# Masked attention loop entered after 14 row maxima instead of 18, with half of the query spreads moved into its steps

## The chip, the cores and the metric

The kernel runs on one core of a Trainium2 chip. The metric is the device time of one execution in microseconds (us), as the median of several runs. The engines named are PE (TensorE), DVE (VectorE), ACT (ScalarE), POOL (GpSimd) and SP (SyncE, which here only issues DMAs).

## The reference, cut to what matters

The program is a two-layer decoder on x of shape (2, 256, 128) with a context of shape (2, 512, 128). Layer 0 is a state-space mixer, a cross attention and a mixture of experts; layer 1 a latent self attention (called "a" in the kernel), a masked cross attention ("x") and a mixture of experts. Each block adds its result to x and normalizes. The change touches the seam of the two attentions of layer 1:

```python
x = layernorm(x + L1_attn(x))                      # "a": 16 heads of 8, 256 keys
# "x": 16 heads of 8, 512 keys, two batch entries
q = einsum('bse,ehd->bhsd', x, Wq) + bq
k = einsum('bse,ehd->bhsd', ctx, Wk) + bk
logits = where(mask, -1e8, einsum('bhsd,bhtd->bhst', q, k))
attn = einsum('bhst,bhtd->bhsd', softmax(logits), v) / sqrt(8)
x = layernorm(x + einsum('bhsd,hdo->bso', attn, Wo) + bo)
```

## The kernel before

Everything is written out by hand: each engine has its own program, and semaphores (`S[...]`) tie them together. An engine waits in the order of its own program, so a wait holds back all that stands behind it. PSUM has 8 banks of 128 x 512 floats.

**The two attention loops.** A loop (`attend_a`, `attend_x` in each engine's program) goes over steps n, a step being 4 heads and 128 keys. In step n PE makes the logits of step n + 1 (keys on partitions, into banks 0 to 3), ACT takes their exponentials (`exp_late`), and PE multiplies the exponentials of step n with the values (`values`, bank 4 or 5). "a" has 16 steps, "x" 32. After the last key tile of a group of 4 heads DVE copies the sum out (`kept`). For "x" PE also adds the mask by two bf16 products with `neg_i` in each half of the logits.

**The maxima.** So that exponentials stay in range, the greatest logit of every query row must be known before the loop reaches its head. PE therefore makes the logits a second time with the queries on partitions (`rows`, one 128x512 matmul for "x"), DVE reduces each to a maximum (`row_max`, for "x" a custom instruction at L1411 that adds the mask and takes the maximum, and a short read of the accumulator). When 8 of these "row" slots of "x" (4 heads of one entry) are done, a "max" slot follows: PE turns the maxima (`max_cols`), ACT copies them negated (`minus_max`), POOL splits them into three bf16 parts (`minus_parts`, 4 instructions), and SP sends each part by DMA into the stacked queries `qs` (`spread_max`). `logits` of the first step of that group waits for the three DMAs. "x" has 64 row slots r0 to r63 and 8 max slots m0 to m7; m0 is for steps 0 to 3, m1 for steps 4 to 7, and so on.

**Where the slots stand.** `first_slots` are those ahead of the loop, 18 rows for "x" (`AHEAD`), in the banks 6, 7, 2, 3 in turn, the last two in 6 and 7; `later_slots` stand in the steps, three to a step until they are used up, in banks 6 and 7 in turn. In a step of "x" PE's order is: slot, half of the logits, slot, other half, slot, values. A slot waits until the one before it in its bank has been read (`fill_slot` and `used`): for a row, until DVE has its maximum. Ahead of the loop each row slot has one identity matmul ahead of it, work without use that keeps PE busy (`idle_work`).

**The spreads.** The queries of "x" are stored as three bf16 parts side by side. `query_parts` (DVE) splits the product of `queries` (PE), 12 small copies per entry (`gather_four`, three by DVE, nine by POOL) bring 4 heads each to the same partitions, and 8 "spreads" per entry (`spread_x`: two 96-row matmuls on PE, one 128x512 copy on ACT) lay two heads each out in `qs`. Entry 0 is batch 0. Before the change all 16 spreads stand ahead of the loop, between its first rows (`spreads_x`), and the loop waits for all.

**The seam.** At the end of loop "a", entry 0 has been attended and normalized (`a_summed(0)`, `a_scaled(0)`, POOL's `root`); entry 1's last heads are copied out, turned (`out_rows`), divided (`normed_rows`), turned again (`attended_cols`), multiplied with Wo (`attended_rows`), summed with the residual (`a_summed(1)`), normalized (`a_scaled(1)`) and turned for the query product (`half_cols("a", 1)`, `queries(1)`). `SECOND` names the row slots of "x" beside which the later pieces of entry 1 stand, `BESIDE` the steps of a loop beside which the pieces of entry 0 stand, `TURNED` the step at which entry 0's attended heads are turned and divided. After the loop of "x" comes the expert layer.

The line of the matmuls is L1666 for all (the helper `mm`).

## Time and profile before

| | us |
|---|---|
| runs (3) | 461.35, 462.95, 464.19 |
| median | 462.95 |
| the profiled execution | 461.53 |
| its span, first to last instruction | 459.7 |

1.83 us of the profiled execution lie outside its span. In a timeline row the columns are: start, length, engine, line, operation, result <- operands, (partitions*columns of the weights) elements and type, how many instructions are merged; in brackets how long the engine stood idle before and what released it. The length of a matmul includes its way through the array, so the starts of neighbouring rows give PE's pace. "PEld" is the load of weights, which overlaps the matmuls.

### The profile page before, as it was taken

The page shows a single profiled execution, that of the slowest core. Times are in us where ns is not written, and L with a number is a line of the kernel's source. Part 1 is how long each engine was busy: PE and PEld are TensorE (multiplying, and loading weights), DVE is VectorE, ACT ScalarE, POOL GpSimd, SP SyncE. Part 2 cuts the span into 40 slices and gives each one's busy share as a digit, 9 for nine tenths or more (in the row PEclk, how much of TensorE's full clock was granted, in tenths as well). Part 3 has the DMA queues.
Part 4 walks back from the last instruction along what each step waited for, and adds up shares of the span by engine and source line. Part 5 has one row for each costly group of instructions (what it writes and reads, how often), then busy time and mean ns, then how long its engine had stood idle before and what let it go on. Part 6 is the DMA issues. An engine that isn't in the chain of part 4 may idle for free.

```text
span 459.7 us, 7702 instructions
## 1 busy us (share of the span) xinstructions
PE 414.8 (90%) x2878; PEld 273.4 (59%) x2886; DVE 294.2 (64%) x688; ACT 206.1 (45%) x290; POOL 185.9 (40%) x237
## 2 busy tenths in 40 slices
PE   4898999999999999798999986789869999999985
PEld 4676645444554447475799864544546555658975
DVE  4779976777666675431622788464688886246644
ACT  1676623233333333115423376457346554566550
POOL 3316647787676766310050465421263332200000
PEclk9989999999999999989999999799999999999998
DMA  8712000000004111160054004300000000000000
GB/s 314 287 37 79 1 0 2 1 1 0 1 1 182 47 46 47 54 223 7 1 133 62 2 0 66 45 3 3 0 1 3 2 2 3 2 13 25 0 1 23
DMA packets 8080, 19.78 MB, mean 43 GB/s; under 512 B 1958, under 2 KB 3974, under 8 KB 7526
## 3 DMA queue, kind: packets, MB, share of 16 engines
q1 hardware_dynamic: 8044, 19.30, 14.3%
q8 instruction: 23, 0.38, 0.3%
q14 instruction: 13, 0.11, 0.1%
HBM read 17.26 MB, written 1.15 MB: 40 GB/s over the span
## 4 chain that ended last, share of the span: by engine, by line
PE 65%; DVE 15%; issue 5%; POOL 5%; DMA 5%; ACT 3%; another core or an unknown queue 0%; SPq 0%; POOLq 0%; DVEq 0%; ACTq 0%
PE ps L1666 63%; DMA late<-mid 4%; DVE ps L1411 3%; DVE big L1215 2%; POOL big L695 2%; DVE ps L1210 2%; DVE mx_a L1415 1%; DMA ident<-in_ident 1%; DVE big L1287 1%; POOL big L702 1%; DVE big L1278 1%; PE ps L1678 1%; POOL big L651 1%; PE ps L2115 1%; ACT late L1061 0%
## 5 line engine op out<-in xcount | busy, mean ns | idle before, releaser
L1666 PE MATMUL ps<-big,late 128*32 128x256 f32 (+3 forms) x760 | 96.7, 383 | 3.0 <-DVE mx_a L1415 1.5
L1666 PE MATMUL ps<-late,big 128*128 128x128 f32 (+1 forms) x448 | 65.6, 277 | 2.6 <-DMA late<-mid 1.9
L955 ACT ACTIVATE big<-ps 128x1024 f32<-128x1024 f32 x48 | 49.1, 1024 | 39.8 <-PE ps L1666 39.6
L894 ACT ACTIVATE big<-ps 128x1024 f32<-128x1024 f32 x32 | 32.8, 1025 | 65.2 <-PE ps L1666 56.8
L1666 PEld LDWEIGHTS ps<-big,late 128*32 128x32 f32 (+2 forms) x768 | 35.0, 116 | 41.4 <-issue 18.4
L1666 PEld LDWEIGHTS ps<-late,big 128*128 128x128 f32 (+1 forms) x448 | 47.2, 152 | 20.1 <-issue 13.3
L695 POOL TENSOR_TENSOR big<-big 128x512 f32<-128x512 f32 x32 | 41.1, 1285 | 28.1 <-DVE big L1287 28.1
L1287 DVE TENSOR_SCALAR big<-big 128x1024 f32<-128x1024 f32 x32 | 27.7, 866 | 33.2 <-ACT big L894 33.2
L1411 DVE CUSTOM_DVE_ANT_0 ps<-ps,big 128x512 f32<-128x512 f32 x64 | 42.7, 708 | 6.9 <-remote 3.2
L630 POOL TENSOR_SCALAR vareps<-meanvar 128x2 f32<-128x2 f32 (+2 forms) x13 | 3.0, 228 | 104.5 <-DVE meanvar L1109 100.7
L1666 PE MATMUL ps<-ident 128*128 128x128 f32 x194 | 28.3, 290 | 7.1 <-DMA ident<-in_ident 6.5
L917 ACT ACTIVATE big<-ps 128x512 f32<-128x512 f32 x32 | 18.9, 597 | 34.0 <-PE ps L1666 34.0
L1666 PE MATMUL ps<-ctx_r,attn_w 128*128 128x512 f32 x64 | 32.6, 618 | 0.7 <-ACT late L861 0.7
L1666 PEld LDWEIGHTS ps<-ident 128*128 128x128 f32 x194 | 26.3, 206 | 8.1 <-DMA ident<-in_ident 6.5
L1666 PE MATMUL ps<-xT,late 128*128 128x256 f32 (+1 forms) x96 | 29.9, 452 | 1.3 <-ACT big L917 1.3
L1666 PE MATMUL ps<-attn_w,ctx_r 128*128 128x128 f32 (+1 forms) x192 | 29.7, 289 | 0.4 <-ACT late L968 0.3
L1666 PE MATMUL ps<-attn_w,big 128*128 128x128 f32 x192 | 26.5, 285 | 2.9 <-DVE big L1279 2.3
L1278 DVE RECIPROCAL big<-ps 128x256 f32<-128x256 f32 x16 | 28.0, 1748 | 1.3 <-PE ps L1666 1.3
L1666 PEld LDWEIGHTS ps<-attn_w,ctx_r 128*128 128x128 f32 (+1 forms) x192 | 23.9, 171 | 7.6 <-issue 2.9
L651 POOL TENSOR_TENSOR big<-big,mid 128x512 f32<-128x512 f32 x16 | 20.4, 1274 | 19.7 <-DVE big L1215 19.7
L1666 PEld LDWEIGHTS ps<-attn_w,big 128*128 128x128 f32 x192 | 24.3, 197 | 5.9 <-DVE big L1279 2.8
L1666 PE MATMUL ps<-big,mid 64*128 64x256 f32 x192 | 27.2, 402 | 0.0
(261 smaller groups left out, 721.2 us busy)
## 6 DMA issues: line engine op xcount, KB each, us to landing
attn_w<-in_w_x SPq DMA_DIRECT2D x1, 2560.0 KB, 12.4
big<-parts_kx SPq DMA_DIRECT2D x18, 128.0 KB
late<-in_w_up SPq DMA_DIRECT2D x1, 2048.0 KB, 7.5
late<-in_w_dn SPq DMA_DIRECT2D x4, 512.0 KB, 4.0
attn_w<-in_w_up SPq DMA_DIRECT2D x1, 1024.0 KB, 7.7
attn_w<-in_w_dn SPq DMA_DIRECT2D x1, 1024.0 KB, 10.1
big<-mid SPq DMA_DIRECT2D x24, 32.0 KB, 1.8
parts_kx<-ctx_r SPq DMA_DIRECT2D x1, 768.0 KB, 3.2
```

The lines of the kernel that those rows point to most:

```text
L651: nc.gpsimd.tensor_tensor(hC[:, s % 8, :], hs[:, s % 4, :], Cn[:], ALU.mult).then_inc(S["hC_done"], 1)
L695: nc.gpsimd.tensor_tensor(esum[:, s, :].rearrange("p (r t) -> p r t", r=2), e[:, :, 0, :], e[:, :, 1, :], ALU.add).then_inc(S["e0_sum"], 1)
L702: nc.gpsimd.tensor_tensor(etot[:, b, :], esum[:, 0, :], esum[:, 1, :], ALU.add).then_inc(S["e0_tot"], 1)
L894: nc.scalar.activation(ex[:, n % 3, :].rearrange("p (r n) -> p r n", r=2), ps[:, 2 * (n % 2):2 * (n % 2) + 2, :], ACT.Exp).then_inc(S["e0_ ...
L917: nc.scalar.activation(dst, ps[:, up_bank0(k, c), :], ACT.Gelu).then_inc(S["up0_act"], 1)
L955: nc.scalar.activation(ex1[:, n % 3, :].rearrange("p (r n) -> p r n", r=2), ps[:, 2 * (n % 2):2 * (n % 2) + 2, :], ACT.Exp, scale=scale).t ...
L1210: nc.vector.tensor_tensor(dBx, dBx, Bn[:], ALU.mult).then_inc(S["dBx_done"], 1)
L1215: nc.vector.tensor_tensor_scan(hs[:, s % 4, :], dA[:, s % 2, :], dBx, 0.0, ALU.mult, ALU.add).then_inc(S["scan_done"], 1)
L1278: link(nc.vector.reciprocal(dst, ps[:, 4 + b, T:2 * T]))
L1287: nc.vector.tensor_scalar(ex[:, n % 3, :], ex[:, n % 3, :], float(np.exp(CLIP)), float(np.exp(-CLIP)), ALU.min, ALU.max).then_inc(S["e0_cl ...
L1411: nc.vector.tensor_tensor_reduce(ps[:, bank, :], ps[:, bank, :], mq[:, 2 * b + q, :], 1.0, -FAR, ALU.add, ALU.max, dst).then_inc(S[f"{L}_r ...
L1666: return nc.tensor.matmul(o, lhsT, rhs, start=start, stop=stop, skip_group_check=shared)
```

## The change

It does these things:

- 14 rows of "x" stand ahead of the loop in place of 18, and m0 with them; m1 moves into step 1. The others go into the steps at the same rate as before.
- Entry 1's 8 spreads stand in the loop, one as the first slot of each of the steps 0 to 7, in bank 6 or 7; the first 8 stay ahead of it. Steps 0 to 7 so have 4 slots. The slots' banks still go 6, 7, 6, 7.
- At the end of loop "a", entry 0's chain to its query (`half_cols("a", 0)`, `queries(0)`, `query_parts(0)`) goes ahead of entry 1's last heads. Entry 1's pieces go beside the first rows of "x": `attended_cols` at row 1, `attended_rows` and `a_summed` at row 3, `half_cols` and `a_scaled` at row 5, `queries` at row 7, `query_parts` at row 8. The 8 identity matmuls ahead of the first spread are gone.
- POOL splits m0 ahead of the nine gathers of entry 1 and not behind them, and it adds the residual's bias behind these.
- Later in loop "x" entry 0's pieces move: turned at step 21 (19), `aT` 22 (20), `y` 23 (21), `xT` 25 (24), router 26 (25).

```diff
-        AHEAD = {"a": 16, "x": 18}
+        AHEAD = {"a": 16, "x": 14}
...
-                if L == "x" and m % row_steps(L) == 1 and m > 1:
+                if L == "x" and m % row_steps(L) == 0 and m:
                     slots.append(("max", m // row_steps(L) - 1))
...
+                if L == "x" and n < H // 2:
+                    slots.append((n, ("spread", H // 2 + n)))
...
-        TURNED = {"a": 9, "x": 19}
-        BESIDE = {"a": {"aT": 11, "y": 12}, "x": {"aT": 20, "y": 21, "xT": 24, "router": 25}}
+        TURNED = {"a": 9, "x": 21}
+        BESIDE = {"a": {"aT": 11, "y": 12, "xT": 15}, "x": {"aT": 22, "y": 23, "xT": 25, "router": 26}}
...
-            return [m - 2] if 8 <= m < AHEAD["x"] else [2 + m // 2] if m % 2 else []
+            return [2 + m // 2] if m % 2 and m < H - 4 else []
...
-        SECOND = {"xT": 1, "q": 3, "parts": 5}
+        SECOND = {"aT": 1, "y": 3, "xT": 5, "q": 7, "parts": 8}
...
             root("post3_0")
             gather_four("qx", 0, 1)
+            gather_four("qx", 0, 2)
             root("post3_1")
-            gather_four("qx", 0, 2)
             gather_four("qx", 0, 3)
+            minus_parts("x", 0)
             pool.wait_ge(norm_out, normed_tiles("post3_1"))
-            nc.gpsimd.tensor_tensor(resid[:], x[:], rv4("bo1"), ALU.add).then_inc(S["res_ready"], 1)
-            pool.wait_ge(S["res_ready"], 5)
             for f in (1, 2, 3):
                 gather_four("qx", 1, f)
-            for k in range(groups("x")):
+            nc.gpsimd.tensor_tensor(resid[:], x[:], rv4("bo1"), ALU.add).then_inc(S["res_ready"], 1)
+            for k in range(1, groups("x")):
                 minus_parts("x", k)
...
@ attend_x, PE
-                half_cols("a", 0)
-                out_rows("a", 1, (H // 4 - 1,))
                 queries(0)
-                attended_cols("a", 1)
-                attended_rows("a", 1)
-                idle_work(2, 8)
                 pe.wait_ge(S["a_o_sb"], 2 * (H // 4))
                 for n in spreads_x(-1):
                     spread_x(n, 4 + n % 2)
+                out_rows("a", 1, (H // 4 - 1,))
...
-                pe.wait_ge(S["x_spread"], H)
+                pe.wait_ge(S["x_spread"], H // 2)
...
@ DVE
                     if n == B * (H // 4) * KEYS["a"] // P - 1:
                         a_scaled(0)
+                        query_parts(0)
                     kept("a", n)
...
             attend_a()
-            query_parts(0)
-            a_summed(1)
             attend_x(1.0 / float(np.sqrt(np.float32(DH))))
```

PE at the end of loop "a", step 15, before. `ident,mid` are `out_rows`, `big2,late` the values, `ident,x` is `half_cols`, `xT,w_x1` `queries`, `ident,x2` `attended_cols`, `w_a1,w_mix` `attended_rows`, `attn_w,ctx_r` a spread, `big1,late` a row.

```order
L2115 MATMUL ps<-ident,mid 128x128 x6
L1666 MATMUL ps<-big2,late 32x256 x4
L2143 MATMUL ps<-ident,x 128x128 x2
L2115 MATMUL ps<-ident,mid 128x128 x2
L1666 MATMUL ps<-xT,w_x1 128x256
L2124 MATMUL ps<-ident,x2 128x128 x2
L1666 MATMUL ps<-w_a1,w_mix 128x128 x2
L1666 MATMUL ps<-ident 128x128 x8
L1666 MATMUL ps<-attn_w,ctx_r 128x256 x4
```

The same place after the change.

```order
L2154 MATMUL ps<-ident,x 128x128 x2
L2126 MATMUL ps<-ident,mid 128x128 x6
L1673 MATMUL ps<-big2,late 32x256 x4
L1673 MATMUL ps<-xT,w_x1 128x256
L1673 MATMUL ps<-attn_w,ctx_r 128x256 x4
L2126 MATMUL ps<-ident,mid 128x128 x2
L1673 MATMUL ps<-ident 128x128
L1673 MATMUL ps<-big1,late 128x512
```

`half_cols` has moved ahead of the first six turns and the values; the first spreads are ahead of entry 1's last two turns.

PE in step 0 of loop "x" before: three rows, and `late,big1` with `sel,neg_i` are a half of the logits.

```order
L1666 MATMUL ps<-big1,late 128x512
L1666 MATMUL ps<-late,big1 128x256 x2
L1666 MATMUL ps<-sel,neg_i 128x256 x2
L1666 MATMUL ps<-big1,late 128x512
L1666 MATMUL ps<-late,big1 128x256 x2
L1666 MATMUL ps<-sel,neg_i 128x256 x2
L1666 MATMUL ps<-big1,late 128x512
L1666 MATMUL ps<-big2,late 32x256 x4
```

Step 0 after the change.

```order
L1673 MATMUL ps<-attn_w,ctx_r 128x256 x2
L1673 MATMUL ps<-late,big1 128x256 x2
L1673 MATMUL ps<-sel,neg_i 128x256 x2
L1673 MATMUL ps<-big1,late 128x512
L1673 MATMUL ps<-late,big1 128x256 x2
L1673 MATMUL ps<-sel,neg_i 128x256 x2
L1673 MATMUL ps<-big1,late 128x512 x2
L1673 MATMUL ps<-big2,late 32x256 x4
```

The spread has the place of the first row, and the last two slots stand side by side.

POOL around the splits, before: `attn_w<-ctx_r` are gathers (three to a call), `resid` the residual's bias, then the split of m0 and of m1.

```order
L630 TENSOR_SCALAR vareps<-meanvar 128x2
L632 TENSOR_TENSOR rstd<-vareps,neghalf 128x2
L730 COPY attn_w<-ctx_r 32x256 x6
L781 TENSOR_TENSOR resid<-x,rowv 128x512
L730 COPY attn_w<-ctx_r 32x256 x9
L742 CAST mid<-mid 4x256
L744 TENSOR_TENSOR mid<-mid 4x256
L745 CAST mid<-mid 4x256
L747 TENSOR_TENSOR mid<-mid 4x256
```

After.

```order
L632 TENSOR_SCALAR vareps<-meanvar 128x2
L634 TENSOR_TENSOR rstd<-vareps,neghalf 128x2
L732 COPY attn_w<-ctx_r 32x256 x3
L744 CAST mid<-mid 4x256
L746 TENSOR_TENSOR mid<-mid 4x256
L747 CAST mid<-mid 4x256
L749 TENSOR_TENSOR mid<-mid 4x256
L732 COPY attn_w<-ctx_r 32x256 x9
L786 TENSOR_TENSOR resid<-x,rowv 128x512
```

The split of m0 is ahead of nine gathers.

## Rows read from the trace of the kernel before

**Rows 1.** The page, part 4: the chain that ended last.

```profile
PE 65%; DVE 15%; issue 5%; POOL 5%; DMA 5%; ACT 3%; another core or an unknown queue 0%; SPq 0%; POOLq 0%; DVEq 0%; ACTq 0%
```

**Rows 2.** Windows: stretch and length, busy of PE, PEld, DVE, ACT, POOL, clock, DMA.

```profile
326.50:332.50 6.00, 4.52 (x32) 3.66 (x34) 4.78 (x17) 1.46 (x4) 1.40 (x4) 1.00 0.00 0
...
341.00:345.00 4.00, 1.74 (x14) 1.50 (x16) 3.96 (x13) 1.28 (x4) 3.44 (x10) 1.00 0.00 0
...
350.16:367.72 17.56, 17.20 (x153) 9.21 (x153) 15.08 (x44) 9.38 (x11) 6.29 (x12) 1.00 0.01 3
```

**Rows 3.** Timeline of PE, end of loop "a" to the first spread.

```profile
324.66 0.88 PE L2115 MATMUL ps<-ident,mid 128*128 128x128 f32 x6
...
327.00 0.65 PE L1666 MATMUL ps<-xT,w_x 128*128 128x256 f32 x2
...
331.39 0.60 PE L1666 MATMUL ps<-attn_w,ctx_r 96*128 96x256 bf16 x4
```

**Rows 4.** Timeline of DVE, the seam up to the first row maximum.

```profile
324.95 0.60 DVE L1119 TENSOR_SCALAR x<-summed,meanvar,rstd 128x128 f32<-128x128 f32 x2 [0.69 <-POOL rstd L632]
326.24 0.42 DVE L1441 COPY mid<-ps 128x256 f32<-128x256 f32 x1 [0.69 <-PE ps L1666]
...
328.01 0.47 DVE L1132 TENSOR_SCALAR ctx_r<-ps,vec 128x256 bf16<-128x256 f32 x1
...
330.88 0.43 DVE L1448 TENSOR_TENSOR summed<-ps,resid 128x256 f32<-128x256 f32 x1
...
333.01 0.70 DVE L1411 CUSTOM_DVE_ANT_0 ps<-ps,big 128x512 f32<-128x512 f32 x1 [0.91 <-remote]
```

**Rows 5.** Timeline of DVE, then PE: r15 and r17 share bank 6.

```profile
347.46 0.73 DVE L1411 CUSTOM_DVE_ANT_0 ps<-ps,big 128x512 f32<-128x512 f32 x1
...
349.05 0.70 DVE L1411 CUSTOM_DVE_ANT_0 ps<-ps,big 128x512 f32<-128x512 f32 x1
```

**Rows 6.** Timeline of PE: r17 with its identity, first logits, values of two later steps.

```profile
348.31 0.49 PE L1666 MATMUL ps<-ident 128*128 128x128 f32 x2
348.63 0.38 PE L1666 MATMUL ps<-big,late 128*128 128x512 bf16 x1
...
349.29 0.38 PE L1666 MATMUL ps<-late,big 128*128 128x256 bf16 x2
...
389.16 0.64 PE L1666 MATMUL ps<-big,late 128*32 128x256 f32 x8
...
390.71 0.64 PE L1666 MATMUL ps<-big,late 128*32 128x256 f32 x8
```

**Rows 7.** Chain of waits, from a negated maximum to the logits that need it.

```profile
314.73 0.37 ACT mid L1011
...
317.50 1.76 DMA late<-mid
...
319.40 0.60 PE ps L1666 x4
```

**Rows 8.** Timeline of ACT, then POOL: two spreads copied, exponentials of step 0; nine gathers, then the split.

```profile
331.81 1.08 ACT L1002 ACTIVATE late<-ps 128x512 bf16<-128x512 f32 x2 [2.81 <-PE ps L1666]
...
350.36 1.02 ACT L955 ACTIVATE big<-ps 128x1024 f32<-128x1024 f32 x1 [0.24 <-PE ps L1666]
...
340.77 4.03 POOL L730 COPY attn_w<-ctx_r 32x256 bf16<-32x256 bf16 x9 [3.39 <-DVE ctx_r L1137]
```

**Rows 9.** Timeline of PE, then DVE: m7, entry 0's pieces in loop "x".

```profile
387.98 0.38 PE L2038 MATMUL ps<-ident,mx_x 128*4 128x128 f32 x2 [0.42 <-DVE mx_x L1411]
...
395.12 0.44 PE L2124 MATMUL ps<-ident,x 128*128 128x128 f32 x2 [0.36 <-DVE x L1428]
...
397.59 0.43 DVE L1529 TENSOR_TENSOR summed<-ps,resid 128x256 f32<-128x256 f32 x1 [2.53 <-PE ps L1666]
```

**Rows 10.** Windows, columns as in rows 2: two stretches at the start of loop "a".

```profile
296.00:298.00 2.00, 0.46 (x4) 0.30 (x4) 0.69 (x1) 0.30 (x2) 1.43 (x3) 0.73 0.00 0
298.00:300.00 2.00, 2.00 (x11) 1.34 (x9) 0.06 (x1) 1.34 (x2) 1.89 (x3) 0.50 0.02 4
```

More of the change, by code:

```diff
@@ L1023, in attend_x @@
                         spread_x(n, 4 + n % 2)
+                    if i == SECOND["aT"]:
+                        attended_cols("a", 1)
                     if i == SECOND["xT"]:
@@ L1030, in attend_x @@
                             minus_max("x", i, bank)
+                    for (kind, i), bank in slots_beside("x", n):
+                        if kind == "spread":
+                            spread_x(i, bank)
                     if n == BESIDE["x"]["aT"] + 1:
@@ L1499, in attend_x @@
                         row_max("x", i, bank)
+                        if i == SECOND["y"]:
+                            a_summed(1)
                         if i == SECOND["xT"]:
@@ L2015, in used @@
                     pe.wait_ge(S[f"{L}_redmax"], i + 1)
+                elif kind == "spread":
+                    pe.wait_ge(S["x_spread"], i + 1)
                 else:
@@ L2063, in fill_slot @@
                     rows(L, i, bank)
+                elif kind == "spread":
+                    spread_x(i, bank)
                 else:
@@ L2193, in attend_a @@
                         attended_cols("a", 0)
+                    if n == BESIDE["a"]["xT"]:
+                        half_cols("a", 0)
                     if n == total - 1:
@@ L2202, in attend_x @@
                 total = B * (H // 4) * KEYS["x"] // P
-                half_cols("a", 0)
-                out_rows("a", 1, (H // 4 - 1,))
                 queries(0)
-                attended_cols("a", 1)
-                attended_rows("a", 1)
-                idle_work(2, 8)
                 pe.wait_ge(S["a_o_sb"], 2 * (H // 4))
@@ L2220, in attend_x @@
                             spread_x(n, 4 + n % 2)
+                        if slot[1] == SECOND["aT"]:
+                            attended_cols("a", 1)
+                        if slot[1] == SECOND["y"]:
+                            attended_rows("a", 1)
                         if slot[1] == SECOND["xT"]:
```

## The prediction

> **What bounds the kernel now.** I read the page first: PE holds 65% of the chain that ended last [rows 1], so what counts is what PE has to wait for or to do more. Then the windows around the change. From 326.5 to 332.5 PE is busy 4.52 of 6.00 us, and 2 us of that are the 8 identity matmuls; from 341 to 345 it is busy 1.74 of 4.00 while DVE is busy 3.96 [rows 2]. So the stretch ahead of loop "x" goes at DVE's pace, a row maximum each 0.65 us. From 350.16 to 367.72 PE is busy 17.20 of 17.56 [rows 2]: these are steps 0 to 7 of loop "x", 17.56 / 8 = 2.195 us each, and there PE itself sets the pace. Steps with no slot are 390.71 - 389.16 = 1.55 us long [rows 6], so a slot costs PE (2.195 - 1.55) / 3 = 0.215 us. The change takes work and DVE time out of a stretch where PE waits and puts slots into one where PE is full. Last I read the timelines of PE and DVE at the seam and around r17, since they show the two turn-rounds used below.
>
> Two latencies. A row begun on PE at 348.63 is taken up by DVE at 349.05, 0.42 later [rows 5, 6]. The maximum of r15 began on DVE at 347.46; r17, in the same bank, was released by it, and its identity began on PE at 348.31, 0.85 later [rows 5, 6]. A bf16 row needs its weights loaded after the release, about 0.1 more (the identity and r17 lie 0.32 apart where their work is 0.22), so I take 0.93. From one row to the next in the same bank PE thus needs 0.42 + 0.93 = 1.35 us at least. Ordinary steps hardly feel this: slot 1 and slot 3 lie a row and two halves of logits apart, 2 x 0.215 + 2 x 0.435 = 1.30 (0.87 us is a step's logits, 350.16 - 349.29 from [rows 2, 6]).
>
> **Entry to loop "x".** Half_cols now stands where the six turns began, at 324.66 [rows 3]. It needs entry 0's rows, which DVE writes from 324.95 for 0.60 us [rows 4]; PE is through at about 325.85, then come the six turns (0.81) and the values (0.57), and the query product starts at about 327.2, against 327.00 [rows 3]. It takes 0.65, so DVE splits the query from 327.9, against 328.01 [rows 4]: the chain put first gains nearly nothing. Split and gather last until 330.88 in the row before, 2.87 us, now until 330.8; then the copy of entry 1's last heads, 0.42 [rows 4], and the first spreads start at 331.2, against 331.39 [rows 3]. They take 0.43, the last two turns 0.44. Before, the turns were issued by 327.00 and their division was over by 328.01, 1.0 us; so it is over at 333.1, and only then can DVE take r0. It took r0 at 333.01 [rows 4]. The eight identity matmuls (8 x 0.22) thus leave a wait, not time.
>
> From r0 on DVE has four row maxima less (-4 x 0.65 = -2.6) and the sum and statistics of entry 1 more (from 330.88 to 332.10, where the idle time ahead of r0 starts [rows 4]: +1.2). The stall behind the normalization of entry 1 stays. New: the last two slots are forced to banks 6 and 7, so r12 follows r11 in bank 6 with nothing between them. Before, r17 followed r15 with r16 between, and DVE took them up 1.59 apart [rows 5], which is 0.3 beyond two maxima; r12 comes 1.59 behind r11, 0.94 beyond one: +0.65. Sum -0.75, and with r0 0.1 later the last row is taken up near 348.4 instead of 349.05. But r17 was followed by a spread and m1 ahead of the first logits, and r13 is issued while DVE is still on r12. First logits at 349.29 before [rows 6], now about 347.7: **-1.6 us**. m0 does not hold them: it is made once r7 is reduced, near 341.4, its split no longer stands behind the 4.03 us of gathers [rows 8], and from the negated copy to the logits it is 319.40 - 314.73 = 4.67 us [rows 7], so they would be free at 346.5. Bounds of this term: 0 (if the 0.3 of the seam go wrong and DVE stalls twice more) and -3.0 (r0 a microsecond sooner, no wait at r12; then m0 is next).
>
> **In the steps.** (1) Eight spreads, four rows and m1 are 13 slots more: 13 x 0.215 = **+2.8**. PE is full there, nothing hides them.
>
> (2) In steps 0 to 7 slots 2 and 4 share a bank, and between their starts lie slot 2 itself, one half of the logits and slot 3: 0.215 + 0.435 + 0.215 = 0.87, against 1.35 needed. PE stands 0.48 before slot 4, in every one of these steps whatever it holds, since m1 and m3 wait for slot 2's maximum too. In step 0 the wait is another: ACT takes the exponentials of step 0 first, which begin 0.2 after the first slot (350.36 to 350.16) and last 1.02, and then copies the spread, 0.54 [rows 8]; slot 3 needs that copy, so it starts at about 1.85 in place of 1.30. That is 0.55, and 0.2 more at the start of step 1. Sum 7 x 0.48 + 0.75 = **+4.1**. Bounds: 0, since the same turn-round of 1.35 over 1.30 leaves no stall in [rows 2] (0.36 idle in 8 steps) and a 4-slot step is in no row; and 7 x 0.75 + 0.75 = 6.0, if DVE takes slot 2 half a maximum late each time. I stay by 0.48, since r17 shows it directly.
>
> (3) m1 moves from ahead of the loop to the last slot of step 1, and step 3 makes the first logits that need it. PE gets there 0.215 (m1) + 0.675 (values, 1.55 - 0.87) + 2.195 + 0.215 + 0.48 (step 2) + 0.215 (slot 1) = 4.0 us after it begins m1. The path needs 0.42 to ACT, some 0.1 behind an exponential, and the 4.67 of [rows 7]: 5.2. **+1.2**, all on PE, with DVE, ACT and the slots behind it queued. Bounds: 0 and 1.6. Later maxima have 2.75 steps or more.
>
> (4) At the end of the slots. m7 waited 0.42 for r63 [rows 9]; now it has a step to itself: **-0.4**. Entry 0's turned heads waited 0.36 [rows 9] because a copy of finished heads stands before the division in step 19; in step 21 there is none: **-0.35**. But `y` at step 23 puts such a copy ahead of the sum: the sum now waits for the values of step 23 (0.57) and the copy (0.42), 0.95 later than at 397.59 [rows 9], and half_cols has two steps instead of three. By the old offsets PE arrives 3.1 us after the sum may begin and its second tile was ready 3.05 after it; with the delay PE waits **+0.9**. Bounds -0.8 and +1.0 for all three. The router's chain ends a step later, ahead of matmuls that PE reaches 2 us after; 0.
>
> **Sum.** -1.6 + 2.8 + 4.1 + 1.2 - 0.4 - 0.35 + 0.9 = **+6.6 us**. The profiled execution took 461.53, 1.83 over its span: 468.1. It lies 1.4 below the median of the runs, 462.95; the mean of the four is 462.5, and on that the sum gives 469.1. I say **469.0**. Ends: -3.0 + 2.8 - 0.8 = -1.0 and 0 + 2.8 + 6.0 + 1.6 + 1.0 = +11.4.
>
> **The clock.** PE now idles from about 327.8 to 331.2, with no identity matmuls in between. Against a loss: from 341 to 345 it was busy 1.74 of 4.00 and the granted clock stayed at 1.00, 2.4 GHz [rows 2]. For it: with 0.46 us of work from 296 to 298 the clock fell, and from 298 to 300 it was 0.50, 1.2 GHz [rows 10]. So a fall is possible in the new gap. It would double spreads, turns, identity and r0 (0.43 + 0.44 + 0.44), about +1.3, the later rows being DVE's. The Trainium skill (TensorE: Matmul & The Clock Gate, "What's actually happening") says that the throttled state is the default and activity lifts it; by that rule this gap costs the 1.3, and the identity matmuls taken out had a use.
>
> **Rivals.** A, my sum: 469.0.
> B, the fourth slot is cheap: the wait of (2) does not show on PE, as the 1.35 over 1.30 does not now; only the slots, the m1 wait and the rest: -1.6 + 2.8 + 1.2 + 0.15 = +2.5, 465.0. For it: in the 8 steps PE idles only 0.36. Against: 0.48 is far more than 0.05.
> C, the clock falls in the seam: 469.0 + 1.3 = 470.3.
> D, not slower: the entry is what matters. If DVE meets no wait at r12 and takes r0 at 332, the loop is entered 3.0 earlier, at 346.3, and if slot 4 then also hides and neither m1's split nor half_cols is waited for: -3.0 + 2.8 - 0.75 = -0.95, 461.5 on the mean. It decides from an entry before 346.5 with steps 0 to 3 no longer than 2.45 us. For it: the 341 to 345 window, where PE idles 2.26. Against: it needs waits to vanish that [rows 5, 7] price.
>
> Chances: A 0.57, B 0.18, C 0.13, D 0.12. A range of 464.5 to 472.5 leaves out D's end and the high bound. About 1%, 4.6 us, is what a measurement here can tell from no change. A clears it but for its low tail (0.07), C clears it, B mostly not (0.03 of it does): slower 0.50 + 0.13 + 0.03 = 0.66; faster 0.03 from D's tail; the rest, 0.31, within.
>
> **What would show it.** In the trace after: first logits of "x" near 347.7; steps 1, 2, 4 to 7 about 2.89 us long with an idle PE of 0.4 to 0.5 before each fourth slot, released by DVE's maximum; a gap of about 1.2 in step 3 released by the DMA of m1; half_cols of entry 0 in step 25 waiting 0.9. I am wrong if PE stays busy over 95% in steps 0 to 7 (then B or D), if the first logits come before 346.5 (D), or if the granted clock is below 1 between 330 and 336 (C).

## The result and the profile after

| | before | after |
|---|---|---|
| median of the runs in one session | 463.57 us | 472.38 us |
| ratio | | 1.0212, interval 1.0135 to 1.0289 |
| the profiled execution / its span | 461.53 / 459.7 | 472.9 / 471.1 |

The change makes the kernel slower. The ratio is one of means (473.2 over 463.4 us): 2.1%, 9.8 us, or 8.6 without the run of 476.67; the medians lie 8.8 us apart. I had said slower, at 469.0, in a range that ended at 472.5. The median is at the very end of that range, and by the ratio the 462.95 from which I forecast becomes 472.8, beyond it. Executions far above the others of the same kernel (such as 1031.58 us in e11) are left out of all ratios here. The page of the profile of the kernel after, the clock by slices and the chain that ended last:

```profile
PEclk9999999999999999899999998799889999999999
...
PE 62%; DVE 13%; DMA 6%; POOL 6%; issue 5%; ACT 5%; SPq 1%; another core or an unknown queue 0%; DVEq 0%; POOLq 0%; ACTq 0%
```

The answer to [rows 1] is that PE holds less of the chain, 62% against 65%, and DVE too, 13% against 15%; ACT went from 3 to 5%, DMA and POOL from 5 to 6% each. I cut both executions at the same places (us from the start of the span), to see where the 11.4 us of the two spans lie:

| | before | after | difference |
|---|---|---|---|
| start of the span to the split of entry 0's query on DVE | 328.01 | 329.63 | +1.6 |
| from there to the first `neg_i` product of loop "x" | 21.49 | 23.50 | **+2.0** |
| from there to the first product with `w_sh`, behind the loop | 65.22 | 72.97 | **+7.75** |
| from there to the end | 45.0 | 45.0 | 0 |

The first difference is upstream of the change, and has two parts. The granted clock, which falls at the start of loop "a" in both kernels [rows 10], stayed at 0.50 longer: from 300 to 302 it was 0.50 after and 0.92 before, and by 307 the kernel after was 0.8 behind. Then a DMA landed later (2.74 us against the 1.76 of [rows 7]), which makes it 1.73. PE's timeline of the kernel after, the row that answers to the 319.40 of [rows 7]:

```profile
321.13 0.60 PE L1673 MATMUL ps<-late,big 128*128 128x256 bf16 x4 [1.30 <-DMA late<-mid]
```

It doesn't belong to the change: in a second execution of the same kernel (below, e10) the query split began at 328.17. From 1.73 at this row to 1.62 at the split the query chain, put first, gained 0.1, as forecast. The other two differences do. In these rows matmuls are L1673 (L1666 before), row maxima L1417 (L1411), turned maxima L2047 (L2038), `half_cols` L2154 (L2143).

**The entry.** The windows of the kernel after around the seam and around r12 (columns as in [rows 2]: busy time of each engine, granted clock, DMA):

```profile
330.00:332.00 2.00, 0.00 (x0) 0.00 (x0) 1.85 (x6) 0.00 (x0) 0.39 (x1) 1.00 0.00 0
332.00:334.00 2.00, 1.01 (x8) 0.97 (x8) 0.99 (x4) 0.58 (x2) 1.75 (x5) 0.91 0.00 0
334.00:336.00 2.00, 1.78 (x9) 1.44 (x8) 1.87 (x7) 0.51 (x2) 0.21 (x1) 0.50 0.00 0
336.00:338.00 2.00, 2.00 (x13) 1.70 (x13) 1.09 (x5) 0.94 (x3) 0.00 (x0) 0.73 0.00 0
...
350.00:352.00 2.00, 1.16 (x4) 1.01 (x5) 0.78 (x4) 0.00 (x0) 1.67 (x6) 0.68 0.00 0
352.00:354.00 2.00, 2.00 (x11) 1.29 (x10) 1.51 (x4) 0.00 (x0) 1.21 (x1) 0.50 0.00 0
```

Twice PE does nothing for more than 3 us, and both times the granted clock is 0.50, 1.2 GHz, in the windows behind. A third stretch between them, 2.11 us ahead of `half_cols`, left it at 1.00. PE's timeline of the kernel after shows the three in the brackets, and the pace behind the last:

```profile
332.99 0.61 PE L1673 MATMUL ps<-attn_w,ctx_r 96*128 96x256 bf16 x4 [3.47 <-DVE mid L1447]
...
341.54 0.79 PE L2154 MATMUL ps<-ident,x 128*128 128x128 f32 x2 [2.11 <-DVE x L1125]
...
350.84 0.80 PE L1673 MATMUL ps<-ident 128*128 128x128 f32 x2 [4.23 <-DVE mx_x L1417]
351.43 0.63 PE L1673 MATMUL ps<-big,late 128*128 128x512 bf16 x1
...
352.28 0.63 PE L1673 MATMUL ps<-big,late 128*128 128x512 bf16 x1
...
353.13 0.63 PE L1673 MATMUL ps<-sel,neg_i 128*128 128x256 bf16 x2
```

A row with its identity takes 352.28 - 351.43 = 0.85 here, where it takes 0.43 at 2.4 GHz: more than the 0.65 of a maximum, so PE, and not DVE, sets the pace. The clock was still down when the loop began: from the first `neg_i` to the first spread of step 0 it is 354.28 - 353.13 = 1.15, against 350.16 - 349.50 = 0.66 before, so 0.5 of the +7.75 is the clock too. The last stretch is as long as it is because DVE is late too. DVE's timeline of the kernel after, the split and the gathers of entry 1's query:

```profile
344.95 0.48 DVE L1138 TENSOR_SCALAR ctx_r<-ps,vec 128x256 bf16<-128x256 f32 x1
...
345.98 0.70 DVE L1141 CAST ctx_r<-cv 128x256 bf16<-128x256 f32 x1
346.71 0.55 DVE L1143 TENSOR_TENSOR ctx_r<-cv,ctx_r 128x256 bf16<-128x256 f32 x1
347.29 1.47 DVE L1150 COPY attn_w<-ctx_r 32x256 bf16<-32x256 bf16 x3
348.68 0.68 DVE L1417 CUSTOM_DVE_ANT_0 ps<-ps,big 128x512 f32<-128x512 f32 x1
```

POOL's timeline of the kernel after, at the same time:

```profile
345.39 0.39 POOL L744 CAST mid<-mid 4x256 bf16<-4x256 f32 x1 [3.07 <-ACT mid L1012]
345.86 0.66 POOL L746 TENSOR_TENSOR mid<-mid 4x256 f32<-4x256 f32 x1
346.59 0.39 POOL L747 CAST mid<-mid 4x256 bf16<-4x256 f32 x1
347.05 0.72 POOL L749 TENSOR_TENSOR mid<-mid 4x256 bf16<-4x256 f32 x1
```

DVE's timeline of the kernel before, the same cast, product and copies:

```profile
339.88 0.29 DVE L1135 CAST ctx_r<-cv 128x256 bf16<-128x256 f32 x1
340.21 0.43 DVE L1137 TENSOR_TENSOR ctx_r<-cv,ctx_r 128x256 bf16<-128x256 f32 x1
340.67 1.02 DVE L1144 COPY attn_w<-ctx_r 32x256 bf16<-32x256 bf16 x3
```

The chain takes 348.68 - 344.95 = 3.73 us, 0.97 more than before. The cast, 0.29 before, is over only after POOL's second instruction. The copies, 1.02 before, where POOL's gathers ran beside them [rows 8], take 1.47 with the first of them beside POOL's fourth. The change put m0's split ahead of the gathers, and so beside this chain. The Trainium skill (SBUF — State Buffer, "SBUF: two separate sides") says that VectorE, in some kinds of instruction, and GpSimd share a pair of ports by an exclusive lock, held for a whole instruction. The cast of 0.70 in place of 0.29 and the copies of 1.47 in place of 1.02 agree with it; no run here shows the port itself.

**The steps.** PE's timeline of the kernel after, steps 0 and 1, the gap of step 3, step 5, and `half_cols` in step 25 (`attn_w,ctx_r` is the spread with which a step starts):

```profile
354.28 0.38 PE L1673 MATMUL ps<-attn_w,ctx_r 96*128 96x256 bf16 x2
...
356.05 1.17 PE L1673 MATMUL ps<-big,late 128*128 128x512 bf16 x10 [0.29 <-ACT late L1003]
357.29 0.39 PE L1673 MATMUL ps<-attn_w,ctx_r 96*128 96x256 bf16 x2
...
362.86 0.39 PE L1673 MATMUL ps<-attn_w,ctx_r 96*128 96x256 bf16 x2
364.24 0.38 PE L1673 MATMUL ps<-late,big 128*128 128x256 bf16 x2 [0.98 <-DMA late<-mid]
...
369.58 0.39 PE L1673 MATMUL ps<-attn_w,ctx_r 96*128 96x256 bf16 x2
...
371.48 0.96 PE L1673 MATMUL ps<-big,late 128*128 128x512 bf16 x9 [0.20 <-DVE mx_x L1417]
372.37 0.39 PE L1673 MATMUL ps<-attn_w,ctx_r 96*128 96x256 bf16 x2
...
414.70 0.58 PE L2154 MATMUL ps<-ident,x 128*128 128x128 f32 x2 [0.72 <-DVE x L1125]
```

A step with four slots and without another wait is 372.37 - 369.58 = 2.79 long. Four slots beside 1.55 of other work would make 2.41, so the fourth costs 0.38 of waiting, though the bracket names only 0.20: the record of the matmul before, 0.38 long at a pace of 0.22, covers another 0.16. Step 0 is 357.29 - 354.28 = 3.01 long, 0.60 over 2.41. The gap of m1 is 364.24 - 362.86 - 0.22 = 1.16. The last row is the wait of `half_cols` in step 25, 0.72.

### The profile page after: what moved, and what is told of

Read it like the earlier page. It is cut to its first block, busy times and chain, and to the rows that moved or that the text cites. A ratio compares the mean times of both kernels' runs of the same rounds, so it can differ in the third digit from the quotient of the medians.

```text
span 471.1 us, 7658 instructions
## 1 busy us (share of the span) xinstructions
PE 416.6 (88%) x2854; PEld 271.5 (58%) x2862; DVE 295.8 (63%) x688; ACT 205.7 (44%) x290; POOL 185.6 (39%) x237
## 3 DMA queue, kind: packets, MB, share of 16 engines
HBM read 17.26 MB, written 1.15 MB: 39 GB/s over the span
## 4 chain that ended last, share of the span: by engine, by line
PE 62%; DVE 13%; DMA 6%; POOL 6%; issue 5%; ACT 5%; SPq 1%; another core or an unknown queue 0%; DVEq 0%; POOLq 0%; ACTq 0%
PE ps L1673 60%; DMA late<-mid 4%; DVE ps L1417 3%; POOL big L697 2%; DVE big L1221 1%; SPq L560 1%; DVE mx_a L1421 1%; DVE ps L1216 1%; DMA big<-mid 1%; DMA ident<-in_ident 1%; POOL big L704 1%; POOL rstd L634 1%; DVE big L1293 1%; PE ps L1685 1%; PE ps L2126 1%
## 5 line engine op out<-in xcount | busy, mean ns | idle before, releaser
L1673 PE MATMUL ps<-big,late 128*32 128x256 f32 (+3 forms) x760 | 98.5, 387 | 3.9 <-DVE mx_a L1421 1.5
L1673 PE MATMUL ps<-late,big 128*128 128x128 f32 (+1 forms) x448 | 66.5, 280 | 4.8 <-DMA late<-mid 4.2
L1673 PEld LDWEIGHTS ps<-late,big 128*128 128x128 f32 (+1 forms) x448 | 47.7, 153 | 22.5 <-issue 14.4
L1673 PEld LDWEIGHTS ps<-big,late 128*32 128x32 f32 (+2 forms) x768 | 35.4, 117 | 41.9 <-issue 18.4
L1417 DVE CUSTOM_DVE_ANT_0 ps<-ps,big 128x512 f32<-128x512 f32 x64 | 43.1, 706 | 15.4 <-PE ps L1673 13.4
L1673 PE MATMUL ps<-ident 128*128 128x128 f32 x170 | 26.0, 300 | 10.5 <-DMA ident<-in_ident 6.0
L1673 PE MATMUL ps<-ctx_r,attn_w 128*128 128x512 f32 x64 | 32.6, 618 | 0.7 <-ACT late L863 0.7
L1673 PE MATMUL ps<-attn_w,ctx_r 128*128 128x128 f32 (+1 forms) x192 | 28.7, 281 | 3.9 <-DVE mid L1447 3.5
L1673 PEld LDWEIGHTS ps<-ident 128*128 128x128 f32 x170 | 24.6, 215 | 12.0 <-DMA ident<-in_ident 6.0
L1673 PE MATMUL ps<-xT,late 128*128 128x256 f32 (+1 forms) x96 | 29.9, 452 | 1.2 <-ACT big L919 1.2
L1673 PEld LDWEIGHTS ps<-attn_w,ctx_r 128*128 128x128 f32 (+1 forms) x192 | 21.9, 162 | 13.5 <-DVE mid L1447 3.9
L744 POOL CAST mid<-mid 4x256 bf16<-4x256 f32 (+1 forms) x12 | 4.6, 387 | 63.4 <-ACT mid L1012 63.4
L1673 PE MATMUL ps<-attn_w,big 128*128 128x128 f32 x192 | 26.5, 285 | 2.9 <-DVE big L1285 2.3
L1673 PEld LDWEIGHTS ps<-attn_w,big 128*128 128x128 f32 x192 | 24.3, 197 | 5.9 <-DVE big L1285 2.8
```

What stands on the lines that cost most here:

```text
L1417: nc.vector.tensor_tensor_reduce(ps[:, bank, :], ps[:, bank, :], mq[:, 2 * b + q, :], 1.0, -FAR, ALU.add, ALU.max, dst).then_inc(S[f"{L}_r ...
L1673: return nc.tensor.matmul(o, lhsT, rhs, start=start, stop=stop, skip_group_check=shared)
```

## The experiments

Each run was compared with the kernel before on the same chip; "entry" is the time from the query split to the first `neg_i`, "loop" from there to the first `w_sh` product (21.49 and 65.22 before, 23.50 and 72.97 after). Diffs are against the kernel after unless said.

**e1: identity matmuls in two of the entry's gaps.**

```diff
                 queries(0)
+                idle_work(2, 15)
...
+                    if slot == ("row", 12):
+                        idle_work(0, 18)
                     fill_slot("x", slot, bank, 1)
```

> The changed kernel with 15 identity matmuls ahead of the first spreads and 18 ahead of r12, that is in the two gaps of 3.5 and 4.2 us in which PE stood idle and behind which its clock was granted at 0.50. Theory 'the clock': without the falls the first rows, r12, r13 and the first logits go at full pace; from r0 to r6 8.17 us fall to about 6.8, from r11 to r12 2.11 to 1.6, from r12's start on DVE to step 0 2.18 to about 0.9, in all 2.5 to 3.3 us less, clock 1.00 from 330 to 356. Rival 'latencies': the matmuls themselves hold the chain, the entry stays within 0.5 us, whatever the clock.

Measured: 468.78, ratio 1.0133 (1.0082 to 1.0183). r0 to r6 took 7.20 us instead of 8.17, r11 to r12 1.58 instead of 2.11; entry 22.42. The clock kept to 1.00 from 328 to 336 and from 348 on, but fell in a gap that I had left. The windows of e1 (PE alone):

```profile
338.00:340.00 2.00, 0.63 (x4) 1.00 0.00 0
340.00:342.00 2.00, 2.00 (x10) 0.51 0.00 0
```

PE's timeline of e1, the row that ends that gap, which is `half_cols` of entry 1:

```profile
339.25 0.78 PE L2154 MATMUL ps<-ident,x 128*128 128x128 f32 x2 [2.24 <-DVE x L1125]
```

The gap was 2.24 us long. The clock is one cause. With two gaps filled it fell behind the third, where a stretch of 2.11 had left it up in the kernel after.

**e2: in those of steps 0 to 7 that have no maxima slot one row fewer, so that they have three slots.**

```diff
+                if L == "x" and n < H // 2 and not ready:
+                    rate = 2
```

> The changed kernel with two rows beside each of the spreads of steps 0 to 7 in place of three, so that six of the eight steps have 3 slots; rows end two steps later. Theory 'fourth slot': 0.37 us of wait go from each of the six, and the rows moved behind cost 0.215 each wherever they stand: steps 2 to 4, 6 and 7 take 2.2 instead of 2.79, and the loop as a whole is 2 us shorter. Rival 'only the slots count': the loop as a whole stays the same within 0.5 us, since the number of slots is the same.

Measured: 475.81, ratio 1.0284 (1.0231 to 1.0338); loop 77.5. I had missed what rows in later steps do to the maxima. The waits of PE in loop "x", e2 (line waited at, releaser: us in total, times, longest):

```profile
PE ps L1675 <- DMA late<-mid: 5.3, 3, 2.1
```

Three maxima now come late and cost 5.3 us of waiting, and a fourth waits 1.4 for ACT. So rows can't be thinned there. The steps themselves did what the theory said: in PE's timeline of e2 the three-slot step 4 goes from 363.09 to 365.30, 2.21, and step 5, with four slots, on to 368.07, 2.77. The fourth slot costs 0.59 in all, 0.22 of work and 0.37 of waiting.

**e3: 16 rows ahead of the loop.**

```diff
-        AHEAD = {"a": 16, "x": 14}
+        AHEAD = {"a": 16, "x": 16}
```

> The changed kernel with 16 rows ahead of the loop, so that m1 is in step 0 and not in step 1. Theory 'm1 is late': the wait of 1.16 us for its DMA in step 3 goes, two rows more ahead of the loop cost DVE 1.3 us there, two slots less in it give 0.43 back: -0.3 us, with the gap of step 3 gone. Rival: the gap moves to another wait of step 3 and the time grows by 0.9 us.

Measured: 469.60, ratio 1.0147 (1.0102 to 1.0192); loop 72.04, entry 24.0. PE has no wait for a DMA left in the loop: m1's wait is gone (-0.98), and the entry is 0.5 longer with the two rows. As the clock was down in the entry here too, this 0.5 is a rough price.

**e4: POOL holds m0's split back until DVE has split the query.**

```diff
             gather_four("qx", 0, 3)
+            pool.wait_ge(S["x_q_parts"], 2 * PARTS)
             minus_parts("x", 0)
```

> The changed kernel, where POOL waits until DVE has split entry 1's query before it splits m0. In the changed kernel DVE's split and gather of that query took 3.8 us and not 2.8, while POOL split m0. Theory 'POOL slows DVE': they take 2.8 again, r9 to r13 come 1.0 us earlier, and m0 just holds the first logits or not, so the entry is 0.5 to 1.0 us earlier. Rival 'the slowing has another cause': DVE's pieces stay at 3.8 us, and the entry is the same or later.

Measured: 470.06, ratio 1.0159 (1.0104 to 1.0214); entry 22.86. DVE's timeline of e4:

```profile
345.21 0.29 DVE L1142 CAST ctx_r<-cv 128x256 bf16<-128x256 f32 x1
345.54 0.43 DVE L1144 TENSOR_TENSOR ctx_r<-cv,ctx_r 128x256 bf16<-128x256 f32 x1
346.00 1.30 DVE L1151 COPY attn_w<-ctx_r 32x256 bf16<-32x256 bf16 x3
```

Cast and product are back at the 0.29 and 0.43 of before; only the copies, beside which POOL's split now runs (from 346.09), stay long, 1.30. Chain 3.05 instead of 3.73. That POOL slows DVE here is shown. The entry's 22.86 says less, since the clock also fell only once in e4's entry, and was up at r12.

**e5: both causes of the entry removed.** All three gaps filled, and e4's wait.

```diff
+            pool.wait_ge(S["x_q_parts"], 2 * PARTS)
...
+                idle_work(2, 15)
...
+                    if slot == ("row", 12):
+                        idle_work(0, 14)
...
                         if slot[1] == SECOND["xT"]:
+                            idle_work(0, 9)
                             half_cols("a", 1)
```

> The changed kernel with identity matmuls in all three gaps of the seam (15 ahead of the first spreads, 9 ahead of half_cols of entry 1, 14 ahead of r12), and POOL's split of m0 behind DVE's split of entry 1's query. Theory 'clock and POOL made the entry late': with the clock at 1.00 from 328 to 356 and DVE's pieces of the query at 2.9 us, the time from DVE's split of entry 0's query to the first masked product of the logits falls from 23.5 to about 20.7 (21.5 in the kernel before); the whole is 2.5 us below the changed kernel, about 468.5, and so still slower than before by the loop's 7. Rival 'the order of the seam itself is slow': it stays above 22.

Measured: 467.48, ratio 1.0103 (1.0032 to 1.0173). Entry 20.43, loop 72.46. The windows of PE in e5:

```profile
328.00:332.00 4.00, 3.88 (x36) 1.00 0.00 0
332.00:336.00 4.00, 3.97 (x31) 1.00 0.01 4
```

With the clock up and POOL away from cast and product (the copies still take 1.31) the entry is 1.06 shorter than before the change. The loop keeps +7.2, with steps of 2.79 and m1's wait of 0.99.

**e6: the spreads of the steps in banks 5 and 4,** where idle values banks are, so that slots 2 and 4 share a bank no longer.

```diff
-                    + [(n, s, 6 + i % 2) for i, (n, s) in enumerate(later_slots(L))])
+                    + [(n, s, 5 - n // 4 % 2) for n, s in later_slots(L) if s[0] == "spread"]
+                    + [(n, s, 6 + i % 2) for i, (n, s) in
+                       enumerate([x for x in later_slots(L) if x[1][0] != "spread"])])
...
```

To keep the order right some spreads move as well: the one of step 4 stands at the end of its step, and the values of steps 4 and 8 wait for the spreads.

> The changed kernel with the spreads of steps 0 to 7 in the bank (5, then 4) in which no values are being summed, so that the other three slots go round banks 6 and 7 as before the change. Theory 'two slots of one bank too near each other': the wait ahead of the last slot goes, ordinary steps take 2.19 + 0.22 = 2.41 us and not 2.79, the stretch from step 0 to step 8 is 2.5 to 3 us shorter; the wait for m1's DMA grows by about 0.4. Rival 'the fourth slot costs by ACT or DVE': steps stay at 2.7 us or more.

Measured: 470.59, ratio 1.0177 (1.0105 to 1.0249); loop 72.02, entry 23.96 with the clock at 0.84 over it. PE's timeline of e6, two neighbouring steps:

```profile
369.73 0.39 PE L1675 MATMUL ps<-attn_w,ctx_r 96*128 96x256 bf16 x2
...
372.14 0.39 PE L1675 MATMUL ps<-attn_w,ctx_r 96*128 96x256 bf16 x2
```

The step is 2.41, the wait before the fourth slot gone. With the three other slots placed as before the change the turn-round no longer shows: it is the shared bank. But the steps now reach m1's queries sooner, and the waits for DMAs grow from 0.98 to 1.9; much of the gain goes there.

**e7: all spreads ahead of the loop,** two beside each of rows 9 and later.

```diff
-                if L == "x" and n < H // 2:
-                    slots.append((n, ("spread", H // 2 + n)))
...
-            return [2 + m // 2] if m % 2 and m < H - 4 else []
+            if m >= 9:
+                return [2 * m - 12, 2 * m - 11]
+            return [2 + m // 2] if m % 2 else []
...
-                pe.wait_ge(S["x_spread"], H // 2)
+                pe.wait_ge(S["x_spread"], H)
```

> The changed kernel with all 16 spreads ahead of the loop again (two beside each of r9 to r13), 14 rows ahead of it, three slots a step. Theory 'the spreads in the steps are the loss': the loop loses 8 slots and 7 waits, 1.7 + 2.9 us, and m1's wait grows to about 2; the entry is later, since the last spreads need POOL's gathers, by 1 to 3 us; in all 1 to 3 us below the changed kernel. Rival: the entry loses all that the loop wins, same time.

Measured: 469.63, ratio 1.0169 (1.0085 to 1.0253); loop 70.55 (-2.4), a DMA wait of 2.2 in it, entry 24.96 with the clock falling again. The steps with three slots are 2.20 again. What they gain, m1's DMA takes in part; behind this wait the clock fell inside the loop as well (0.52 from 366 to 368), and the last gathers, then spreads, stand ahead of the loop. The profiled execution, 473.41, is the slowest of the four, 3.8 above their median.

**e8: the kernel before with 16 rows ahead,** all 16 spreads ahead, and entry 0's later pieces one step later. Diff against before:

```diff
-        AHEAD = {"a": 16, "x": 18}
+        AHEAD = {"a": 16, "x": 16}
...
+            if 14 <= m < AHEAD["x"]:
+                return [2 * m - 16, 2 * m - 15]
```

> The kernel before with two rows less ahead of the loop (16), m1 in step 0, the spreads as before, and entry 0's pieces of loop x one step later (turned beside step 20, its sum beside 22). Theory: DVE sets the pace ahead of the loop, so the entry is 1.3 us earlier, three slots more cost 0.65, the waits of 0.42 ahead of m7 and 0.36 ahead of attended_cols go: 1.4 us faster than before, ratio 0.997. Rival 'm1 comes too late': PE waits for its DMA in step 3 and the gain is gone, ratio 1.000 or above.

Measured: 461.97, ratio 0.9977 (0.994 to 1.0015), which can't be told from no change. Entry 21.13, only 0.36 shorter (I think because spreads stand in front of r15; not shown); loop 65.43. A gain from entering earlier exists, but two rows are worth half a microsecond at most.

**e9: e5, e6 and e3 together.**

> The changed kernel with the three repairs together: identity matmuls in the idle stretches of the entry and POOL held back until DVE has split the query, the spreads of the steps in the other banks (5, then 4), and 16 rows ahead of the loop instead of 14. Theory (the loss is made of the entry's clock and POOL, the fourth slot's turn-round, m1's DMA, and the work itself): entry 20.9 us from the query split to the first neg_i (20.4 of the clean entry plus two maxima less what DVE had spare, +0.5), loop 72.46 - 2.6 (seven waits of 0.37) - 0.3 (step 0) - 1.0 (m1) - 0.4 (two row slots fewer) = 68.2 from first neg_i to first w_sh; median about 464.5, ratio 1.003; what is left of the loop's gap to the kernel before (65.2) is then eight spreads and two rows as work (2.2) and half_cols and later waits (0.8). Rival (the causes hide each other, so the repairs do not add: when steps are shorter, another wait, such as the DMAs of the maxima or the values' wait for the spreads, takes their place): loop 70 or more, median 466 to 467.

Measured: 463.53, ratio 1.0008 (0.998 to 1.0035). Entry 20.83 (20.9 expected), loop 68.33 (68.2 expected). PE's waits in loop "x", e9:

```profile
PE ps L2159 <- DVE x L1128: 0.7, 1, 0.7
...
PE ps L2050 <- DVE mx_x L1420: 0.4, 1, 0.4
```

No wait for a DMA, and none before the fourth slots. The repairs add up, and by the runs they take back the whole loss, to within what can be measured (0.35%, 1.6 us, at most is left). By the two traces e9 is still 2.4 behind: +3.1 in the loop against -0.7 in the entry. The +3.1 is for the most part eleven more slots, eight spreads, two rows and m1 (11 x 0.215 = 2.37), and the wait of `half_cols` (0.7).

**e10: the kernel after once more.** No edit.

> The changed kernel unchanged, once more. Its first profiled execution lay 1.7 us behind upstream of the change (a late DMA of loop a), and its clock fell in two gaps of the entry. Theory (the loss is in the entry's clock, POOL beside DVE's split, the slots and waits of steps 0 to 7): from the query split of entry 0 to the first neg_i 23.5 again, within 0.5, with a granted clock of 0.5 in the two seconds of microseconds behind the first gap, and the loop 72.5 to 73; the query split again near 328.1 as in the other runs, so the median 471 and the ratio near 1.017. Rival (the upstream delay belongs to the change): the query split again at 329.6 and the median at 472.4 or more.

Measured: 472.62, ratio 1.0210 (1.0155 to 1.0265), span 471.0. The query split began at 328.17, as the theory said; but entry 24.25 and loop 73.59 lie above its bounds, and the median above its 471. The windows of e10 (PE alone):

```profile
332.00:334.00 2.00, 1.78 (x9) 0.50 0.00 0
...
342.00:344.00 2.00, 2.00 (x8) 0.50 0.03 8
...
352.00:354.00 2.00, 2.00 (x11) 0.50 0.00 0
```

Here the clock is down in three stretches, and the entry costs 0.75 more than in the first profile; the same kernel at the same total, without the upstream delay. The third fall lasts until 355.2, 2.8 us into the loop. The fall at 342 stands behind the same 2.11 us of idle PE, ahead of `half_cols`, that left the clock up in the first profile. How often the clock falls differs from execution to execution, and the runs without a profile show it too. Each has its mean granted clock on record, and in the four of e10 the time rises as it sinks: 469.42 us at 0.981, 472.45 at 0.971, 472.8 at 0.968, 474.43 at 0.964. The 476.67 of the first session had 0.929. The four of e5 lie at 0.979 to 0.988.

**e11 and e12: the kernel before without the 8 identity matmuls ahead of the first spreads.** Diff against before:

```diff
                 attended_rows("a", 1)
-                idle_work(2, 8)
```

> The kernel before, with nothing changed but the 8 identity matmuls ahead of the first spreads left out. PE is then idle from about 329.6 to 331.4, 1.8 us, behind three short waits, and again 0.5 and 1.3 us afterwards. Theory (the identity matmuls kept TensorE's clock up): the granted clock falls to about 0.5 somewhere between 330 and 336, r0 is then taken up 0.6 to 1.0 us later, and the first neg_i comes about 1 us later: 0.2% slower, median 464. Rival (an idle stretch under 2 us does not lower the clock here, it needs the 3.5 us of the changed kernel): the clock stays at 1.00 from 328 to 338 and nothing moves.

Measured in e11: 464.1 against 462.33, ratio 1.002 (0.999 to 1.0049); its profiled execution took 1031.58 us (see the next text), so e12 ran the same kernel.

> Again the kernel before without the 8 identity matmuls ahead of the first spreads, since the only profiled execution of it took 1031.58 us, its matmuls all at a fraction of their pace, and can't be compared. Theory (the identity matmuls kept the clock up): granted clock below 1 between 330 and 336, and the first neg_i 0.5 to 1 us later than at 349.50. Rival (1.8 us idle does nothing here): clock 1.00 from 328 to 338, first neg_i within 0.2 of 349.50.

Measured in e12: 463.84 against 462.01, ratio 1.0034 (1.0008 to 1.006). The windows of e12 (PE alone):

```profile
328.00:330.00 2.00, 0.71 (x4) 1.00 0.00 0
330.00:332.00 2.00, 1.17 (x8) 0.92 0.00 0
332.00:334.00 2.00, 1.38 (x6) 0.50 0.00 0
...
336.00:338.00 2.00, 2.00 (x8) 0.50 0.00 0
...
346.00:348.00 2.00, 2.00 (x9) 0.50 0.00 1
```

PE's longest wait ahead of the first fall was 1.22 us, and still the clock fell. Entry 24.57, 3.1 more than before; loop 65.22, the same to the hundredth. But the clock fell twice. PE's timelines, of e12 and then of the kernel before, the row of m0's turned maxima:

```profile
344.13 0.38 PE L2038 MATMUL ps<-ident,mx_x 128*4 128x128 f32 x2 [2.51 <-DVE mx_x L1411]
```

```profile
343.21 0.38 PE L2038 MATMUL ps<-ident,mx_x 128*4 128x128 f32 x2 [2.59 <-DVE mx_x L1411]
```

The second fall came behind a wait that the kernel before has as well, there with the clock at 1.00. By r6, behind the first fall, e12 had lost 1.55 (342.53 - 327.38 against 341.61 - 328.01); the other 1.5 came with the second, and one execution can't say whether the missing identity matmuls had a part in that. The runs put the whole at 0.2 to 0.34%, 0.9 to 1.6 us. That the clock falls was forecast, and the first fall alone cost more than the 0.5 to 1 us expected: with the clock down PE needs longer than DVE for each row (0.85 against 0.65), so the loss goes on for as long as the fall, and does not end with the spreads.

## Why the prediction was right or wrong

**The failed step: "Entry to loop x", -1.6 us.** It was +2.0 in the profiled execution and +2.8 in e10. Its own working was near: e5, with the clock at 1.00 and POOL off the cast, has -1.06, and r12 came 1.59 behind r11 (forecast 1.59). Of the 0.5 that is missing 0.3 is a slip: from r13's maximum at 348.4 I went back 0.7 to the first logits at 347.7, where e5 shows 0.38 (348.64 and 348.26). The rest is the copies, still 0.29 longer. What the step lacked:

- The clock. I had taken it out of the sum and priced it as rival C, at 1.3 us and a chance of 0.13. C's own sign showed: the granted clock below 1 between 330 and 336. Its price was too low: e5's entry is 3.07 shorter than that of the kernel after and 3.82 shorter than e10's, and without the 0.68 of POOL some 2.4 and 3.1 are left for the clock (an estimate from these cuts), beside 0.5 and 1.1 at the start of the loop. There are two reasons. I said "the later rows being DVE's", but at 1.2 GHz they are PE's (0.85 a row against 0.65; in e12 the first fall alone cost 1.55). And I looked at the gap in the seam alone, not at the one that my own r12 stall and the query chain make, nor at the one ahead of `half_cols`. The evidence I weighed against it, the window from 341 to 345 of [rows 2], is part of a single idle stretch of 2.59 us. It shows that such a stretch can leave the clock up, but from one execution: behind the 2.51 of e12 it fell. And it says nothing of the 3.4 us that I forecast for the seam. The rule of the Trainium skill that I quoted in the clock's paragraph (TensorE: Matmul & The Clock Gate, "What's actually happening") said what happened: the throttled state is the default, and the identity matmuls had a use. C should have been in the sum.
- POOL. I counted the moved split of m0 as a gain (earlier queries) and did not ask which of DVE's instructions it would run beside: +0.97 on entry 1's query chain, of which e4 gives 0.68 back.

That r0 would gain nothing was right: it is taken up at 334.75 with 1.6 of that upstream, 5.1 behind the query split, against 5.0 before.

**The mechanisms of the steps and the loop were right, their sum 1 us too high.** The sum of all terms behind the entry was 2.8 + 4.1 + 1.2 - 0.4 - 0.35 + 0.9 = +8.25; measured +7.75 (after), +7.2 (e5), +8.4 (e10). Both profiles of the kernel after entered with the clock down, so e5's is the one to compare.

- (2), +4.1: the wait is there in each step, 0.38 instead of 0.48, so 7 x 0.38 plus step 0's 0.60 (forecast 0.75) is some 3.3. e6 shows that the bank is the cause, and the three-slot steps of e2 and e7, 2.20 long, agree. The 1.35 of the turn-round was 0.1 too long. Rival B (cheap fourth slot) is out.
- (3), +1.2 for m1: 1.16. e3 shows that it is only the two rows' place.
- (4): `half_cols` waits 0.72 (forecast 0.9); m7 and the turned heads of entry 0 wait no more, as said.
- (1), +2.8 for 13 slots: not measured alone, but with it the measured terms make 2.8 + 3.3 + 1.16 + 0.72 - 0.4 - 0.35 = 7.2, which is e5's loop.

**The other way round.** Rival D needed an entry before 346.5; even e5, with all clean, had its first `neg_i` at 348.48. The whole loss is by comparison of ratios: 1.0212 after, 1.0103 with the entry repaired (some 5 us), 1.0008 with the steps repaired too (some 4.4 us). These come from three sessions, so each part is known to about 2 us; the cuts of the traces say 3.1 + 0.5 for the first and 4.1 - 0.4 for the second. The first is larger by the runs than by these traces. Against e10's profile, where the clock fell three times, it is 3.8 + 1.1 = 4.9, and the mean clocks of the runs without a profile (e10 above) point the same way. So how often the clock falls can explain the difference.

No version here beats the kernel before by more than can be measured; e8 is the nearest, at 0.9977.

## What to carry to other kernels

Matmuls without use are part of the schedule: before removing some, or opening a wait near them, list every idle stretch of PE that results and price the fall of the clock over the whole series behind it, where the pace may pass from the other engine to PE. One profile is not enough for that: the same stretch left the clock up in one execution and not in the next. Slots moved into a loop are worth what they free ahead of it only if the engine there is the one that they load; spreads cost 0.215 each on a full PE and freed nothing on DVE. Before giving a loop one more slot per step, work out the shared bank's turn-round, and put the new slot where it has a bank of its own.

## What the runs showed of the hardware

- The granted clock fell to 0.50 behind idle stretches of PE of 3.47, 4.23 and 2.24 us, and in e12 behind waits of 0.50, 0.47, 1.22 and 0.47 us in a row, a stretch in which PE was busy 0.71 and 1.17 of 2 us, and behind one of 2.51. In the kernel before it stayed at 1.00 behind a stretch of 2.59, and from 332 to 336 with PE busy 1.04 and 1.08 of 2 us (its windows there). A stretch of 2.11 left it up in one execution of the kernel after, and in the other (e10) it fell behind it. So the same gap may or may not cost.
- Beside four POOL instructions on 4 partitions x 256 a DVE cast of 128 x 256 took 0.70 us in place of 0.29, a product 0.55 in place of 0.43, and three copies of 32 x 256 1.47 in place of the 1.02 that they took beside POOL's copies of 32 x 256.
- From the start of a row to that of the next matmul in its bank, the steps show 0.87 + 0.38 = 1.25 us, against the 1.35 that I had put together from the rows around r17.
